# One filler matmul in front of each unit of maxima in the lead-in of a fused layer, in place of fillers at its end

## The reference

```python
def ffn(x):                     # W_fc (512,128), W_proj (128,512) made ternary, -1, 0 or 1
    h = gelu(x @ ternary(W_fc).T)
    return layernorm(h) @ ternary(W_proj).T
def attn(x):                    # 2048 queries against 2048 keys, 16 heads of width 8
    q, k = rope(proj(x, wq, bq)), rope(proj(x, wk, bk))
    p = softmax(q @ k.T / sqrt(8)); return (p @ v) @ wo.T + bo
x = x + 0.5 * ffn(norm(x)); x = x + attn(norm(x)); x = x + 0.5 * ffn(norm(x))
```

## Time and profile before

| | us |
|---|---|
| median of 3 runs | 767.67 |
| lowest, highest | 766.25, 768.15 |
| profiled execution, its own time | 763.32 |
| its span, first to last instruction | 761.4 |
| mean granted TensorE clock | 0.958 |

### The profile page before, as it was taken

One profiled execution on the slowest core, in us unless ns is written; L12 is line 12 of the kernel. 1 busy time (PEld: TensorE's weight loads), 2 busy tenths in 40 slices (PEclk: granted clock), 3 DMA queues, 4 the chain that ended last, 5 costly groups with the idle time before them and its releaser, 6 DMA issues.

```text
span 761.4 us, 17532 instructions
## 1 busy us (share of the span) xinstructions
PE 722.2 (95%) x6843; PEld 242.9 (32%) x6843; DVE 688.8 (90%) x880; ACT 637.3 (84%) x1196; POOL 256.9 (34%) x526
## 2 busy tenths in 40 slices
PE   5898779999999999999999999999999999999994
PEld 2774211222222222222222222222222222224373
DVE  6678659999999999999999999999999999996374
ACT  3544643999999999999999999999999999999842
POOL 4332001455455445233323332232222222424321
PEclk8999755999999999999999999999999999999998
DMA  7000000000011011011000000000000000000001
GB/s 221 2 1 0 1 0 2 3 5 4 24 25 25 24 25 25 25 24 40 4 4 4 4 4 3 5 19 5 4 4 4 5 6 21 7 7 3 7 15 42
DMA packets 22674, 12.45 MB, mean 16 GB/s; under 512 B 13088, under 2 KB 21152, under 8 KB 22336
## 3 DMA queue, kind: packets, MB, share of 16 engines
q1 hardware_dynamic: 11328, 8.77, 4.1%
q0 software_dynamic: 9056, 2.04, 1.6%
q10 hardware_dynamic: 2208, 0.53, 0.4%
HBM read 7.34 MB, written 2.33 MB: 13 GB/s over the span
## 4 chain that ended last, share of the span: by engine, by line
DVE 63%; PE 28%; issue 4%; ACT 2%; DMA 1%; POOL 0%; SPq 0%; DVEq 0%; POOLq 0%; ACTq 0%
DVE mh L819 59%; PE ps L1339 7%; PE ps L1326 5%; PE ps L1126 3%; PE ps L1307 3%; PE ps L1226 2%; PE ps L1185 2%; PE ps L1202 2%; ACT KT L1031 1%; DVE ring L681 1%; PE ps L1354 1%; DMA X<-in_L_attn_x_dram 1%; DMA QT<-mrow 0%; PE ps L1192 0%; DVE mrow L836 0%
## 5 line engine op out<-in xcount | busy, mean ns | idle before, releaser
L819 DVE TENSOR_REDUCE mh<-ps 128x2 f32<-128x1024 f32 x512 | 584.8, 1213 | 6.3 <-PE ps L1307 6.2
L1082 ACT ACTIVATE ring<-ps 128x512 f32<-128x512 f32 x1024 | 551.2, 600 | 30.6 <-PE ps L1326 15.9
L1339 PE MATMUL ps<-ring,Vx 128*32 128x256 f32 x4096 | 325.4, 392 | 0.9 <-ACT outT L1090 0.9
L1307 PE MATMUL ps<-KT,QT 48*128 48x512 bf16 x1024 | 209.3, 392 | 10.1 <-DVE mh L819 9.7
L1326 PE MATMUL ps<-QT,KT 51*128 51x512 bf16 x1024 | 212.6, 388 | 1.7 <-DMA QT<-mrow 0.6
L1339 PEld LDWEIGHTS ps<-ring,Vx 128*32 128x32 f32 x4096 | 82.0, 108 | 172.0 <-ACT ring L1082 156.4
L1326 PEld LDWEIGHTS ps<-QT,KT 51*128 51x128 bf16 x1024 | 51.9, 93 | 220.6 <-ACT ring L1082 205.6
L549 POOL DMA_DIRECT2D rope<-outT x80 | 42.9, 542 | 147.4 <-ACT outT L1090 139.6
L538 POOL DMA_DIRECT2D QT<-mrow x128 | 71.7, 565 | 42.2 <-DVE mrow L836 38.7
L526 POOL TENSOR_TENSOR mp<-zeros,top 128x8 bf16<-128x8 f32 x32 | 6.3, 198 | 223.3 <-DVE top L827 223.3
L1307 PEld LDWEIGHTS ps<-KT,QT 48*128 48x128 bf16 x1024 | 50.1, 94 | 52.4 <-DVE mh L819 23.8
(11 more groups left out here) (133 smaller groups left out, 344.0 us busy)
## 6 DMA issues: line engine op xcount, KB each, us to landing
rope<-rope_tables SPq DMA_DIRECT2D x2, 1024.0 KB, 6.2
QT<-mrow SPq DMA_DIRECT2D x128, 0.8 KB
QT<-mrow POOLq DMA_DIRECT2D x128, 0.8 KB, 1.7
rope<-outT SPq DMA_DIRECT2D x80, 8.0 KB
rope<-outT POOLq DMA_DIRECT2D x80, 8.0 KB, 1.7
q_bounce<-XB SPq DMA_DIRECT2D x3, 384.0 KB, 2.4
QT<-q_bounce SPq DMA_DIRECT2D x18, 64.0 KB
QT<-q_bounce POOLq DMA_DIRECT2D x18, 64.0 KB, 3.2
```

Source lines behind the costliest of these rows:

```text
L819: v.tensor_reduce(mh[:, n // A_STEP % 2, :, q, kb], ps[:, bank:bank + 2, :], AX.X, ALU.max)\
L1082: a.activation(ring[:, n % PRING, :], ps[:, exp_bank(n), :], ACT.Exp, scale=SCALE).then_inc(p_ready, 1)
L1307: mm = t.matmul(ps[:, A0 + 2 * (n % 2) + h, :], QT[rows, j, at:at + P], KT[rows, j, kb * CS:(kb + 1) * CS], start=True, stop=True)
L1339: mm = t.matmul(ps[r:r + 32, PO, 0:QH], Vx[:, kt, col:col + 32], ring[:, (2 * n + h) % PRING, half * QH:(half + 1) * QH], start=(kt == 0), ...
```

## The change

In front of the matmuls of each unit with index 2 to 24 (the units 3 to 25, counted from one: 23 of them) stands one filler matmul, into the lower one of that unit's own two banks. Because it writes that bank, it waits on the same `a_free` value as the unit does. The unit's own second matmul overwrites what the filler wrote. The eight fillers behind the units with index 17 to 24 are gone.

```diff
             for n in range(LEAD):
+                if n >= 2:
+                    pe.wait_ge(a_free, n - 1)
+                    warm(1, A0 + 2 * (n % 2))
                 max_mm(2 * n)
                 max_mm(2 * n + 1)
...
                 if n == 13:
                     place_half("K3", 1, 1)
-                if n > A_STEP:
-                    warm(1, EXP[1])
```

## The result

| | before | after |
|---|---|---|
| median of 20 runs, us | 764.98 | 767.89 |
| lowest to highest | 763.3 to 768.15 | 764.63 to 773.73 |
| ratio of after to before, 95% interval | | 1.0051 (1.0033 to 1.0068) |
| profiled execution: span, clock | 761.4, 0.958 | 768.9, 0.955 |

The change makes the kernel slower, by about half a per cent. The three runs of before that the forecast stood on had a median of 767.67, while twenty have 764.98. So the measured difference is 2.9 us between the medians and 3.9 by the ratio, where 5.5 were forecast, and 767.89 lies just under the range of 768.9 to 776.8.

What follows compares the result with a forecast made beforehand. The lead-in's chain through PE was taken as what counts, the full main loop merely shifting. Placing stretch 4.1, tail 1.2 and first rounds 0.2 gave 5.5 us on 767.67: 773.2 us, range 768.9 to 776.8.

Steps and rivals of the forecast that it cites:

- A filler costs 0.54 us on the chain, nothing under cover: Lead-in at the half clock: each filler on PE's chain adds 0.54 us, bounds 0.43 and 0.61; in idle time nothing.
- The placing stretch and the tail, +5.3: Lead-in: fillers at indices 2 to 13 add 4.1 us, index 14 to the loop adds 1.2.
- up to index 3: Start of the placing stretch: fillers of index 2 (+0.3 us, full clock) and index 3 (+0.54) stand in the chain.
- The tail's round: Index 14 to 24: a filler inside the bank's round makes two units take 2.48 us instead of 2.26, four times.
- The first rounds, +0.2: Start of the main loop: clock rise may shift, from -0.6 us (wait gone) to +1.7 (two more slow rounds); taken +0.2.
- The ends of my own range: Whole kernel: +3.1 us with 0.43 a filler and early clock, +8.0 with 0.61 and two slow rounds; 770.8 to 775.7.
- The fillers raise the clock in the placing stretch: Rival in the lead-in: clock rises near 107 us, sum -0.5 us, or earlier near 94; 763 to 767; chance 0.08.
- the sign of being wrong that I had named: New profile's lead-in: a 0.50 clock stretch ending before 128 us, or placing steps staying at 1.93 us.
- the wait at the loop's start: First rounds: DVE's wait of 0.60 us at 133.70, which the clock-raising rival took to vanish, -0.6.
- The level: Starting time of the kernel before: 767.67 us, median of three runs, to which the 5.5 us were added.

Runs made afterwards that it cites:

- the covered places: Kernel before plus three fillers only, in front of the units with index 4, 6 and 10, the old eight kept; ratio 1.0001, median 765.32 us.
- the second profile: Changed kernel profiled and run again without any edit, 12 runs beside the kernel before; ratio 1.0032, median 767.16 us.
- the first profile: Profile of the changed kernel from its first measurement against the kernel before; 20 runs, median 767.89 us, ratio 1.0051.
- the higher cluster: The slower 12 of the changed kernel's 32 runs, no edit between them; median 772.5 us, against 766.7 for the other 20.

## Why the prediction came out as it did

- *A filler costs 0.54 us on the chain, nothing under cover*: right. Steps of 2.48 for 1.94, idle times of 0.74 shrunk to 0.20, and the covered places at 0.0 us. At the full clock it was 0.32 (112.42 to 112.74 in the second profile), where I had put 0.3. The rule of the Trainium skill (TensorE: Matmul & The Clock Gate, "What happens when you issue a matmul") by which the next load hides under the running matmul (0.43 us) didn't hold for these 128-row fillers.
- *The placing stretch and the tail, +5.3*: in the first profile the first score matmul comes 49.34 us behind the first unit, 44.79 before: +4.55. I had too much by 0.75: the clock fell later behind the first unit (3.8 us for 3.2), so that up to index 3 only 0.26 us were added where 0.84 were forecast, and the score matmul follows the last unit after 0.40 us, not 0.54. The tail's round was right: reductions 16 to 24 take 9.89 us for 9.23, +0.66, where 0.88 less 0.2 was forecast.
- *The first rounds, +0.2*: mis-sized. The clock came up 9.1 us behind the first score matmul instead of 6.2, and DVE waited at three reductions for 0.49, 0.75 and 0.72 us where it had waited for 0.60 and 0.33. From the first score matmul to reduction 40 it is +1.3. The sum for an execution whose clock doesn't come up before the loop is +5.8 us of lead-in, against 5.5 forecast.
- *The ends of my own range*: the working has slips. With 0.43 a filler the same terms give 0.3 + 7 x 0.43 + 0.43 + 4 x 0.11 - 0.2 = 4.0 and not 3.7, with 0.61 they give 6.1 and not 6.3. Neither moves the forecast.
- *The chances*: this is the step that failed. "The fillers raise the clock in the placing stretch" had 0.08, but by their clocks 20 of 32 runs went that way. I argued from the tail of before, where a filler behind each unit left the clock at 0.50 for 8.7 us, that a thinner mix could do no better. The second profile shows it coming up at 110.4 us, which is also the sign of being wrong that I had named, a stretch of 0.50 that ends before 128. I had priced that rival's sum at -0.5 us; its lead-in measures +1.9. The placing steps came out at 1.39 as priced, but the rise was 3 us later than the 107 assumed, and the clock fell again at 120.7: reductions 16 to 24 took 0.65 us more than before after all, and the wait at the loop's start, which I had as gone, grew (24 to 40 took another 0.63). With these two lead-ins and each set's own split, the first twenty runs (11 and 9) would be +3.7 us by their mean, where the ratio gives 3.9, and the twelve of the repeat (9 and 3) +2.9, where it gives 2.4. Each lead-in is that of one profile.
- *The level*: three runs put before 2.7 us above its twenty-run median. With 764.98 the same sum would have given 770.5 and the range 766.2 to 774.1, which holds 767.89. So it is the level that puts the median outside the range; but with the right level the number would have come close by luck: only 3 of the 32 runs lie within 1 us of 770.5, at the low edge of the higher cluster.
- *Left open*: why an execution goes one way or the other. Both profiles run the same code, the clusters are 5.7 us apart and the lead-ins 3.9; the profile of the higher cluster also reached its first unit 1.8 us later. Whether that goes with the higher cluster in general two profiles can't tell.

## What to carry to other kernels

A filler that keeps TensorE's clock up belongs where PE is idle anyway and what is queued behind it has time; in front of work on the chain it costs its whole length, 0.54 us here, and behind a wait on the very reduction that the next unit needs, it lengthens the round. It can still earn more than that if there are enough of them, as the version with two in front of each unit shows (0.9970). Before pricing a clock from one profile, look at the clocks of all runs: a kernel near the edge goes both ways, and the mean is neither. Where a little filling helps in part of the executions only, try more of it under cover before giving it up.

## What the runs showed of the hardware that I had not expected

- PE busy for 8.55 of 8.70 us left the clock at 0.50, and so did 9.00 of 9.00 us in the first profile of the changed kernel (134.7 to 143.7). In the second one it came up at 110.4 us behind 3.17 of 3.20. Being busy alone doesn't tell. Fillers of 32 rows in the same places had the clock of the higher cluster in eleven of twelve runs.
- A matmul of 32 rows ran beside placings on other rows at no cost to the step (1.94 us with and without), but cost 0.41 us behind placings that use its own rows.
- The clock also dropped for a moment near the end in five of the fourteen profiles. The same stretch in the second one of the changed kernel, where it dropped, and in that of before, where it didn't:

```profile
741.90:745.30 3.40, 3.40 (x18) 3.40 (x17) 2.05 (x8) 0.89 (x2) 1.02 (x1) 0.50 0.00 0
```

```profile
741.90:745.30 3.40, 3.40 (x17) 2.14 (x16) 2.77 (x7) 1.08 (x2) 0.00 (x0) 1.00 0.26 77
```

The five profiles with that drop have a rest of 615.2 to 615.6 us, the nine without it 613.4 to 613.6: 1.7 us from code that no version touched.
